# Cosine attention: softmax denominators in four column quarters of TensorE, their inverses spread by transfers

## The chip, the cores and the metric

One NeuronCore of a Trainium2 chip runs the whole program. The metric is the device time of one execution in microseconds (us), lower is better. The engines of the core have queues of their own and meet at semaphores: TensorE (PE, with its weight loads as PEld), VectorE (DVE), ScalarE (ACT), GpSimd (POOL) and SyncE (SP), whose part here is to issue DMA transfers. A run of matmuls on PE works in program order; an instruction that waits holds back all that is behind it on its engine.

## The reference, cut to what matters

The model is a chain of four attention blocks and four feed-forward blocks on x of 16 sequences x 256 tokens x 128 features, all in f32. The change touches the second attention block alone:

```python
q = (x @ w_q).reshape(b, s, h, -1).transpose(0, 2, 1, 3)
...
q = _l2norm(q) * jnp.exp(scale)
k = _l2norm(k)
sim = jnp.einsum('bhid,bhjd->bhij', q, k)
attn = jax.nn.softmax(sim, axis=-1)
out = jnp.einsum('bhij,bhjd->bhid', attn, v)
out = out.transpose(0, 2, 1, 3).reshape(b, s, h * out.shape[-1])
return out @ w_out + b_out
```

There are 16 heads of 64 features; x is layer-normalised ahead of it and the result is added to x. The softmax is worked without its division: the kernel sums exp(sim - peak) over the keys for each query (the denominator) and divides the value product by it.

## The kernel before

The stage is the function `cosine_attention`. Tokens are taken in 8 groups of 512 (two sequences, s = 0 and 1); heads are taken in pairs (r = 0 and 1), 8 pairs to a group, so there are N = 64 pairs of a head pair and a group. Each is numbered n. A software pipeline runs over a step number i. In step i PE does, in this written order: `project(i,0)` (q of pair i, L704), `norm(i-1)` (sums of squares, L717), `score(i-2,0)` (L730), `project_v(i)` (L710), `score(i-2,1)`, `project(i,1)` (k, L704 again), `values(i-3,0)` and `values(i-3,1)` (L744, and L748 for the denominators), then in some steps `turn_x` (four transposes for the next group, L689) or `project_out` of one output tile (L758, L759). An f32 matmul is two instructions in the trace.

The denominators: `consts["ones"]` is all ones, so the matmul at L748 puts the sum over the keys of `summed` on each of its output rows. For each sequence and head it writes 64 rows (the 64 that the head's values take in O_BANK) by 256 columns, so DEN_BANK holds 128 rows x 512 columns that line up with O_BANK. ACT turns them into inverses by Ln and Exp (`invert_den`, L835 and L837, 128x512 each), and DVE multiplies (`normalize`, L905) into `oT`.

The order on the other engines is written out as well. DVE in step i: `take(i,0)` (copies q out of PSUM, L886), `clamp(i-1)` (L892), `normalize(i-4)`, `take(i,1)`, `unite(i-1)` (multiplies q and k by their inverse norms, two instructions at L899), and in output steps `add_out` (L909). In one step of a group `measure` stands ahead of that (L865 to L872), in the next `normalize_x` (L879). ACT in step i: `invert_norm(i-1)` (L805, L811), `exp(i-2,0)`, `copy_v(i)` (L818), `square(i,0)`, `exp(i-2,1)`, `square(i,1)`, `invert_den(i-3)`, and `copy_x` (L795) after `turn_x`; `root` (L786, L788) stands at the head of a step. SP sends in step i the inverse norms of pair i-1: four transfers, each of 32 rows repeated four times into 128 rows of `inv_all` (L670). POOL adds the two key tiles of `probs` into `summed` (L938).

Three waits tie this together. `values(n,0)` waits for `normalized` >= n, that is for `normalize(n-1)`, since O_BANK and DEN_BANK are single. `project(i,1)` waits for `copy_v(i)`, and `project_v(i)` for `take(i,0)`, since all three projections use A_BANK. `take(i,1)` waits for `project(i,1)`.

## Time and profile before

| what | value |
|---|---|
| median of 3 runs | 6622.44 us (6621.18 to 6631.18) |
| profiled execution, its own time | 6623.76 us |
| its span | 6622.0 us |
| cosine stage, first to last instruction on the engines | about 1095 to 1792 us |
| PE busy over the span | 6003.8 us (91%) |
| DVE, ACT, POOL busy over the span | 4160.9, 3471.2, 2272.1 us |

How to read the rows further down. A row of the timeline is: start in us from the span's start, how long in us, engine, line, operation, output<-inputs, rows and columns, count; in brackets the idle time of the engine just before it and what ended it. Consecutive instructions of one line are merged in a row, so the start of one row and the start of the next give the pace of an engine; the length of a row of matmuls takes in the drain of the last of them. A row of the stretches is the stretch, its length, and busy time with instruction count of PE, PEld, DVE, ACT and POOL, then the granted clock of PE as a share of full speed, the busy share of the DMA engines and GB/s. A row of the groups is line, engine, operation, names, shapes and count, then busy us in total and mean ns of one, then idle time before and its releaser. The stage of the change lies wholly on one core, and its steps repeat, so single steps are read.

### The profile page before, as it was taken

To read this page: it belongs to the slowest core of one execution; us is meant where nothing else is said; L and a number is where in the kernel's file an instruction comes from. 1 tells how busy PE (TensorE), PEld (TensorE's weight loads), DVE (VectorE), ACT (ScalarE), POOL (GpSimd) and SP (SyncE) were. 2 spreads that over 40 slices of the span, in tenths; PEclk is the share of its full clock that TensorE was granted. 3 is DMA by queue.
4 is the path that set the end of the run, shared out by engine and by line. 5 is a ranking of instruction groups with operands and counts; after the bars stand their busy time and mean duration, and the time that the engine had idled before them with its cause. 6 is when DMAs were issued, how large, how long until landed. Compare 5 with 4: busy or idle time off the path is not lost. (4 is left out here: it accounts for less than half of the span.)

```text
span 6622.0 us, 128662 instructions
## 1 busy us (share of the span) xinstructions
PE 6003.8 (91%) x51745; PEld 3325.1 (50%) x51745; DVE 4160.9 (63%) x6986; ACT 3471.2 (52%) x5688; POOL 2272.1 (34%) x1589
## 2 busy tenths in 40 slices
PE   7999988999777777999769999999999999999998
PEld 3555554444442223766435555555555555555554
DVE  2333333444358886332768888888888888788885
ACT  3343323666434443444536666666666666666664
POOL 0111100222114443000035555555555555555553
PEclk9999987999968888999879999999999999999998
DMA  1000000222200000000011111111111111111111
GB/s 55 1 1 1 1 0 16 52 52 52 62 5 0 0 0 0 1 0 0 1 45 33 33 46 37 33 46 37 33 43 40 33 40 40 33 35 46 37 38 27
DMA packets 184105, 175.14 MB, mean 26 GB/s; under 512 B 24181, under 2 KB 174742, under 8 KB 183318
## 3 DMA queue, kind: packets, MB, share of 16 engines
q1 hardware_dynamic: 183542, 167.27, 10.6%
q8 instruction: 397, 6.50, 0.4%
q14 instruction: 166, 1.36, 0.1%
HBM read 30.88 MB, written 2.10 MB: 5 GB/s over the span
## 5 line engine op out<-in xcount | busy, mean ns | idle before, releaser
L2545 POOL TENSOR_TENSOR local_ssum<-local_sq 128x512 f32<-128x512 f32 x384 | 694.1, 1808 | 2149.4 <-ACT local_sq L2333 2148.9
L2553 POOL TENSOR_TENSOR local_rot<-local_rot,local_inv_all 128x512 f32<-128x512 f32 x768 | 963.3, 1286 | 87.4 <-DMA local_inv_all<-local_inv 86.7
L2154 PE MATMUL banks<-local_y,local_Wqkv 128*128 128x512 f32 x1536 | 823.4, 618 | 64.2 <-ACT local_sq L2333 61.4
L2355 ACT ACTIVATE local_probs<-local_probs,local_npeak 128x1152 f32<-128x1152 f32 x384 | 482.7, 1257 | 355.2 <-DVE local_probs L2459 355.2
L2459 DVE TENSOR_TENSOR local_probs<-banks,band 128x576 f32<-128x576 f32 x768 | 546.0, 752 | 184.7 <-PE banks L2189 179.3
L2439 DVE TENSOR_TENSOR local_rot<-banks,local_rotary_scaled 128x512 f32<-128x512 f32 x768 | 525.2, 684 | 192.1 <-PE banks L2154 186.4
L2333 ACT ACTIVATE local_sq<-banks 128x512 f32<-128x512 f32 x768 | 459.4, 598 | 246.6 <-DVE local_sin L2440 238.3
L2349 ACT COPY local_v<-banks 128x512 f32<-128x512 f32 x384 | 224.8, 585 | 594.6 <-PE banks L2167 594.1
L2446 DVE TENSOR_TENSOR local_rot<-local_rot,local_sin 128x1024 f32<-128x1024 f32 x384 | 504.9, 1315 | 40.8 <-DVE local_sin L2440 0.9
L2189 PEld LDWEIGHTS banks<-local_rot 32*128 32x128 f32 x12288 | 415.4, 185 | 225.2 <-issue 198.6
L2440 DVE TENSOR_TENSOR local_sin<-banks,local_rotary_scaled 128x512 f32<-128x512 f32 x768 | 521.8, 679 | 0.0
L2209 PEld LDWEIGHTS banks<-local_probs,local_v 128*32 128x32 f32 x12288 | 346.0, 110 | 302.8 <-issue 292.5
L2189 PE MATMUL banks<-local_rot 32*128 32x160 f32 (+1 forms) x12288 | 488.5, 295 | 0.0
L1261 POOL TENSOR_TENSOR mamba_seen<-mamba_state,mamba_c_wide 128x1024 f32<-128x1024 f32 x128 | 301.0, 2352 | 474.9 <-DVE mamba_state L1342 474.9
L2209 PE MATMUL banks<-local_probs,local_v 128*32 128x160 f32 (+1 forms) x12288 | 459.5, 290 | 0.5 <-DVE local_oT L2467 0.5
L2154 PEld LDWEIGHTS banks<-local_y,local_Wqkv 128*128 128x128 f32 x1536 | 264.3, 190 | 371.7 <-ACT local_sq L2333 247.6
L938 POOL TENSOR_TENSOR cosine_summed<-cosine_probs 128x512 f32<-128x512 f32 x128 | 162.7, 1271 | 738.2 <-ACT cosine_probs L828 738.1
L2167 PE MATMUL banks<-local_Wqkv,local_y 128*128 128x512 f32 x768 | 396.0, 597 | 0.0
L419 POOL TENSOR_TENSOR favor_summed<-favor_probs 128x256 f32<-128x256 f32 x128 | 92.9, 726 | 778.1 <-DVE favor_probs L381 778.1
L2224 PE MATMUL banks<-local_oT,local_Wo 128*128 128x512 f32 x768 | 354.9, 605 | 0.9 <-ACT local_gate L2377 0.9
L1158 PE MATMUL banks<-mamba_seen,ident 128*128 128x512 f32 x512 | 291.1, 697 | 63.7 <-DVE mamba_xs L1349 42.3
L381 DVE TENSOR_TENSOR favor_probs<-banks,causal 128x768 f32<-128x768 f32 x128 | 122.6, 957 | 355.3 <-PE banks L231 355.3
(399 smaller groups left out, 10905.1 us busy)
## 6 DMA issues: line engine op xcount, KB each, us to landing
local_inv_all<-local_inv SPq DMA_DIRECT2D x768, 128.0 KB, 2.7
cosine_inv_all<-cosine_inv SPq DMA_DIRECT2D x256, 128.0 KB, 2.6
local_Wqkv<-in_L_ffn_Wqkv_quads SPq DMA_DIRECT2D x36, 256.0 KB, 2.9
local_Wo<-in_L_ffn_Wo_quads SPq DMA_DIRECT2D x6, 512.0 KB, 4.1
experts_w_W<-in_L_ffn_W SPq DMA_DIRECT2D x1, 2048.0 KB
out<-x SPq DMA_DIRECT2D x8, 256.0 KB, 2.3
local_W<-in_L_ffn_W SPq DMA_DIRECT2D x12, 170.5 KB, 2.3
cosine_w_Wqkv<-in_L_attn_w_kv SPq DMA_DIRECT2D x1, 1024.0 KB
```

What stands on the lines that cost most here:

```text
L2154: pe.matmul(seqs(banks[:, QK_BANK, :]), Wqkv[:, at:at + P], y_group(g), start=True, stop=True).then_inc(qk_projected, 1)
L2167: pe.matmul(banks[:, V_BANK, :], y[:, 2 * g + tile // ST, at:at + P], Wqkv[:, V_COLUMNS(half)], start=True, stop=True).then_inc(v_projecte ...
L2189: last = pe.matmul(banks[:, S_BANK + r, lo:hi], k[rows_r, half, at:at + P], q[rows_r, half, at:at + hi - lo], start=(half == 0), stop=(hal ...
L2209: last = pe.matmul(banks[rows_r, O_BANK, part * SEQ + at:part * SEQ + to], v[:, G % 2, s * ST + tile, c:c + 32], probs[:, e % 3, r, lo:hi] ...
L2333: act.activation(sq[:, c % 2, :], banks[:, QK_BANK, :], ACT.Square).then_inc(squared, 1)
L2355: act.activation(a, a, ACT.Exp, bias=npeak[:, layer:layer + 1], scale=SCALE).then_inc(exped, 1)
L2439: dve.tensor_tensor(seqs(rot[:, k % ROTATED, half, :]), raw, twice(table[:, m, 0, half, :]), ALU.mult).then_inc(cosined, 1)
L2440: dve.tensor_tensor(seqs(sin[:, m, half, :]), raw, twice(table[:, m, 1, half, :]), ALU.mult).then_inc(sined, 1)
L2446: dve.tensor_tensor(a, a, sin[:, k % 2, ::-1, :], ALU.add).then_inc(rotated, 1)
L2459: dve.tensor_tensor(probs[:, e % 3, r:r + 2, :], banks[:, S_BANK + r:S_BANK + r + 2, 0:SCORES], consts["band"].unsqueeze(1).broadcast_to([ ...
L2545: pool.tensor_tensor(ssum[:, n % 2, m, :], sq[:, 0, :], sq[:, 1, :], ALU.add).then_inc(square_summed, 1)
L2553: pool.tensor_tensor(a, a, twice(inv_all[:, n % 2, m, of_seq(s)]), ALU.mult).then_inc(united, 1)
```

## The change

The denominators move out of `values` into a function of their own that PE runs after `values(n,1)`. For each sequence s and head r it makes the product with 32 columns of ones, so 32 rows by 256 columns, and puts them at rows 32 x (2s + r) of DEN_BANK: all four of a pair side by side in the four column quarters of the array, in 256 columns of the bank. ACT makes the inverses on 128x256 instead of 128x512, into `inv_den` (two buffers), and does so one step later in the loop, ahead of `invert_norm`, as `invert_den(i-4)`. SP then spreads them: four transfers for each pair, each reading 32 rows twice into the 64 rows of a head for one sequence of `rden` (two buffers now), ahead of the four that send the inverse norms. DVE's `normalize(i-4)` waits for these transfers, and stands behind `take(i,1)` instead of ahead of it. The wait of PE's `values(n,0)` for `normalize(n-1)` stays as it was. `valued` is now counted once a pair and no longer twice, and the waits on it are renumbered.

```diff
...
-        rden, oT = sb("rden", [P, GN]), sb("oT", [P, OUTS, GN])
+        inv_den, rden, oT = sb("inv_den", [P, 2, SEQ]), sb("rden", [P, 2, GN]), sb("oT", [P, OUTS, GN])
...
+        den_sent = signals(nc, ctx, "cos_den_sent_even cos_den_sent_odd")
...
+                def send_den(n):
+                    sp.wait_ge(den_inverted, n + 1)
+                    if n >= 2:
+                        sp.wait_ge(normalized, n - 1)
+                    for q in range(GB):
+                        for r in range(2):
+                            at = 32 * (2 * q + r)
+                            rows = inv_den[at:at + 32, n % 2, :]
+                            source = bass.AP(rows.tensor, rows.offset, [rows.ap[0], [0, 2], rows.ap[-1]])
+                            sp.dma_start(rden[r * HD:(r + 1) * HD, n % 2, of_seq(q)], source).then_inc(den_sent[n % 2], 16)
+
                 for i in range(FIRST, LAST + 1):
+                    if (n := within(i - 4)) is not None:
+                        send_den(n)
                     if (n := within(i - 1)) is not None:
                         send_inverse(n)
...
-                    for r in range(2):
-                        rows_r = slice(r * HD, (r + 1) * HD)
-                        last = pe.matmul(banks[rows_r, DEN_BANK, of_seq(s)], consts["ones"][:, 0:HD], summed[:, n % 2, s, r, :],
-                                         start=True, stop=True)
+
+                def denominators(n):
+                    for s in range(GB):
+                        for r in range(2):
+                            c = 2 * s + r
+                            last = pe.matmul(banks[32 * c:32 * c + 32, DEN_BANK, 0:SEQ], consts["ones"][:, 0:32], summed[:, n % 2, s, r, :],
+                                             start=True, stop=True)
                     last.then_inc(valued, 1)
...
                     if (n := within(i - 3)) is not None:
                         values(n, 0)
                         values(n, 1)
+                        denominators(n)
                     if (g := group_at(i, 2 - PAIRS)) is not None:
...
-                        act.wait_ge(valued, 2 * PAIRS * (g - 1))
+                        act.wait_ge(valued, PAIRS * (g - 1))
...
-                        act.wait_ge(valued, 2 * n - 2)
+                        act.wait_ge(valued, n - 1)
...
                 def invert_den(n):
-                    act.wait_ge(valued, 2 * n + 2)
-                    if n:
-                        act.wait_ge(normalized, n)
-                    act.activation(rden[:], banks[:, DEN_BANK, :], ACT.Ln).then_inc(den_logged, 1)
+                    act.wait_ge(valued, n + 1)
+                    if n >= 2:
+                        act.wait_ge(den_sent[n % 2], 64 * (n // 2))
+                    a = inv_den[:, n % 2, :]
+                    act.activation(a, banks[:, DEN_BANK, 0:SEQ], ACT.Ln).then_inc(den_logged, 1)
                     act.wait_ge(den_logged, n + 1)
-                    act.activation(rden[:], rden[:], ACT.Exp, scale=-1.0).then_inc(rden_ready, 1)
+                    act.activation(a, a, ACT.Exp, scale=-1.0).then_inc(den_inverted, 1)
 
...
                     if (g := group_at(i, 1 - PAIRS)) is not None:
                         root(g)
+                    if (n := within(i - 4)) is not None:
+                        invert_den(n)
...
-                    if (n := within(i - 3)) is not None:
-                        invert_den(n)
                     if (g := group_at(i, 2 - PAIRS)) is not None:
                         copy_x(g)
...
                 def normalize(n):
-                    dve.wait_ge(rden_ready, n + 1)
+                    dve.wait_ge(den_sent[n % 2], 64 * (n // 2 + 1))
                     if n >= OUTS:
                         dve.wait_ge(out_ready, GT * (group_of(n - OUTS) + 1))
-                    dve.tensor_tensor(oT[:, n % OUTS, :], banks[:, O_BANK, :], rden[:], ALU.mult).then_inc(normalized, 1)
+                    dve.tensor_tensor(oT[:, n % OUTS, :], banks[:, O_BANK, :], rden[:, n % 2, :], ALU.mult).then_inc(normalized, 1)
...
                     if (n := within(i - 1)) is not None:
                         clamp(n)
+                    if within(i) is not None:
+                        take(i, 1)
                     if (n := within(i - 4)) is not None:
                         normalize(n)
-                    if within(i) is not None:
-                        take(i, 1)
                     if (n := within(i - 1)) is not None:
                         unite(n)
...
-                        pool.wait_ge(valued, 2 * (n - 2) + s + 1)
+                        pool.wait_ge(valued, n - 1)
...
```

PE's queue at a plain step in the middle of the stage, before (L748 are the denominators, the wait `normalized` is on the first L744 of `values(i-3,0)`):

```order
L704 MATMUL banks<-cosine_xnT,cosine_w_Wqkv 128x512 [waits v_copied]
L744 MATMUL banks<-cosine_probs,cosine_v 64x256 [waits v_copied,normalized,probs_summed,exped]
L744 MATMUL banks<-cosine_probs,cosine_v 64x256 x3
L748 MATMUL banks<-cosine_summed,ones 64x256 x2
L744 MATMUL banks<-cosine_probs,cosine_v 64x256 [waits v_copied,probs_summed,exped]
L744 MATMUL banks<-cosine_probs,cosine_v 64x256 x3
L748 MATMUL banks<-cosine_summed,ones 64x256 x2
```

The same place on PE now, with the line numbers of the changed file (L718 is `project`, L758 `values`, L765 the denominators):

```order
L718 MATMUL banks<-cosine_xnT,cosine_w_Wqkv 128x512 [waits v_copied]
L758 MATMUL banks<-cosine_probs,cosine_v 64x256 [waits v_copied,normalized,probs_summed,exped]
L758 MATMUL banks<-cosine_probs,cosine_v 64x256 x3
L758 MATMUL banks<-cosine_probs,cosine_v 64x256 [waits v_copied,probs_summed,exped]
L758 MATMUL banks<-cosine_probs,cosine_v 64x256 x3
L765 MATMUL banks<-cosine_summed,ones 32x256 x4
```

The two pairs of 64-row denominators became one run of four with 32 rows behind all values; the first of the values still waits for `normalized`.

DVE's queue for one step, before (L886 is `take`, L892 `clamp`, L905 `normalize`, L899 `unite`):

```order
L886 COPY cosine_qk<-banks 128x512 [waits scored,qk_projected]
L892 TENSOR_SCALAR cosine_ss<-banks 128x256 [waits inverted,norm_summed]
L905 TENSOR_TENSOR cosine_oT<-banks,cosine_rden 128x512 [waits out_ready,rden_ready]
L886 COPY cosine_qk<-banks 128x512 [waits scored,qk_projected]
L899 TENSOR_TENSOR cosine_qk<-cosine_qk,cosine_inv_all 128x512 [waits squared,cos_inv_sent_odd]
```

The same place on DVE now (L905 is `take`, L911 `clamp`, L924 `normalize`, L918 `unite`):

```order
L905 COPY cosine_qk<-banks 128x512 [waits scored,qk_projected]
L911 TENSOR_SCALAR cosine_ss<-banks 128x256 [waits inverted,norm_summed]
L905 COPY cosine_qk<-banks 128x512 [waits scored,qk_projected]
L924 TENSOR_TENSOR cosine_oT<-banks,cosine_rden 128x512 [waits out_ready,cos_den_sent_even]
L918 TENSOR_TENSOR cosine_qk<-cosine_qk,cosine_inv_all 128x512 [waits squared,cos_inv_sent_odd]
```

`normalize` changed places with the second `take` of the step.

## Rows read from the trace of the kernel before

**Rows 1.** A stretch in the middle of the stage.

```profile
1400.00:1500.00 100.00, 94.84 (x612) 50.74 (x608) 40.18 (x75) 60.16 (x104) 23.43 (x19) 1.00 0.21 48
```

**Rows 2.** Groups of instructions by line and form, over the stage.

```profile
L748 PE MATMUL banks<-cosine_summed,ones 128*64 128x256 f32 x512 | 77.3, 380 | 0.0
...
L717 PE MATMUL banks<-cosine_sq,heads_of_pair 128*32 128x256 f32 x512 | 41.8, 398 | 3.0 <-ACT cosine_xnT L795 2.9
```

**Rows 3.** Timeline of a plain step, i = 31, PE, DVE and ACT.

```profile
1414.80 1.12 PE L704 MATMUL banks<-cosine_xnT,cosine_w_Wqkv 128*128 128x512 f32 x2
...
1415.86 0.64 PE L717 MATMUL banks<-cosine_sq,heads_of_pair 128*32 128x256 f32 x8
1415.96 0.69 DVE L886 COPY cosine_qk<-banks 128x512 f32<-128x512 f32 x1 [0.77 <-PE banks L704]
...
1416.42 1.13 PE L730 MATMUL banks<-cosine_qk 64*128 64x256 f32 x8
1416.57 0.42 DVE L892 TENSOR_SCALAR cosine_ss<-banks 128x256 f32<-128x256 f32 x1
...
1417.47 0.51 ACT L811 ACTIVATE cosine_inv<-cosine_ss,cosine_up 128x256 f32<-128x256 f32 x1
...
1419.21 0.58 ACT L818 COPY cosine_v<-banks 128x512 f32<-128x512 f32 x1
...
1419.84 1.12 PE L704 MATMUL banks<-cosine_xnT,cosine_w_Wqkv 128*128 128x512 f32 x2 [0.16 <-ACT cosine_v L818]
...
1420.90 1.08 PE L744 MATMUL banks<-cosine_probs,cosine_v 128*64 128x256 f32 x8
1421.00 0.69 DVE L886 COPY cosine_qk<-banks 128x512 f32<-128x512 f32 x1 [3.42 <-PE banks L704]
...
1421.81 0.60 PE L748 MATMUL banks<-cosine_summed,ones 128*64 128x256 f32 x4
...
1422.24 1.03 PE L744 MATMUL banks<-cosine_probs,cosine_v 128*64 128x256 f32 x8
...
1423.11 0.60 PE L748 MATMUL banks<-cosine_summed,ones 128*64 128x256 f32 x4
...
1423.64 1.13 PE L704 MATMUL banks<-cosine_xnT,cosine_w_Wqkv 128*128 128x512 f32 x2
```

**Rows 4.** Timeline, the output step before it, i = 30.

```profile
1403.57 1.12 PE L704 MATMUL banks<-cosine_xnT,cosine_w_Wqkv 128*128 128x512 f32 x2
...
1412.40 2.05 PE L758 MATMUL banks<-cosine_w_Wo,cosine_oT 128*128 128x128 f32 x16
```

**Rows 5.** Timeline, steps i = 32 to 34, where DVE is late.

```profile
1424.20 1.29 DVE L899 TENSOR_TENSOR cosine_qk<-cosine_qk,cosine_inv_all 128x512 f32<-128x512 f32 x2 [2.50 <-DMA cosine_inv_all<-cosine_inv]
...
1434.34 1.12 PE L704 MATMUL banks<-cosine_xnT,cosine_w_Wqkv 128*128 128x512 f32 x2
...
1436.08 1.11 DVE L879 TENSOR_SCALAR cosine_xn<-x,cosine_moments,cosine_rstd 128x128 f32<-128x128 f32 x4 [1.22 <-ACT cosine_rstd L788]
...
1444.77 1.12 PE L704 MATMUL banks<-cosine_xnT,cosine_w_Wqkv 128*128 128x512 f32 x2
```

**Rows 6.** Timeline and the tile `cosine_inv_all`: the transfers of the inverse norms.

```profile
1438.60 0.51 ACT L811 ACTIVATE cosine_inv<-cosine_ss,cosine_up 128x256 f32<-128x256 f32 x1
...
1443.74 1.55 DVE L899 TENSOR_TENSOR cosine_qk<-cosine_qk,cosine_inv_all 128x512 f32<-128x512 f32 x2 [0.92 <-DMA cosine_inv_all<-cosine_inv]
...
L670 SPq DMA_DIRECT2D cosine_inv_all<-cosine_inv x256: 542/604/1417, 1115.1 to 1761.7; - x128
...
DMA to landing us min/median/max: 2.5/2.6/4.3
```

**Rows 7.** Timeline, the end of the stage, where PE waits for `normalize`.

```profile
1774.67 0.69 DVE L905 TENSOR_TENSOR cosine_oT<-banks,cosine_rden 128x512 f32<-128x512 f32 x1 [8.42 <-ACT cosine_rden L837]
...
1775.51 1.08 PE L744 MATMUL banks<-cosine_probs,cosine_v 128*64 128x256 f32 x8 [2.18 <-DVE cosine_oT L905]
```

**Rows 8.** Timeline of PE in the last stage, after an idle stretch.

```profile
3880.98 1.97 PE L2154 MATMUL banks<-local_y,local_Wqkv 128*128 128x512 f32 x2 [2.12 <-ACT local_sq L2333]
```

More of the change, by code:

```diff
@@ L652, in cosine_attention @@
         sems = (qk_projected, copied, squared, norm_summed, clamped, logged, inverted, unit, v_projected, v_copied, scored, exped,
-                probs_summed, valued, den_logged, rden_ready, normalized, out_ready, added) = signals(
+                probs_summed, valued, den_logged, den_inverted, normalized, out_ready, added) = signals(
             nc, ctx, "qk_projected copied squared norm_summed clamped logged inverted unit v_projected v_copied scored exped "
-            "probs_summed valued den_logged rden_ready normalized out_ready added")
+            "probs_summed valued den_logged den_inverted normalized out_ready added")
         inv_sent = signals(nc, ctx, "cos_inv_sent_even cos_inv_sent_odd")
+        den_sent = signals(nc, ctx, "cos_den_sent_even cos_den_sent_odd")
         tiles = lambda g: x[:, g * GT:(g + 1) * GT, :]
@@ L943, in _ @@
                         sum_probs(n, s)
-        restart(nc, [*first, *norms, *sems, *inv_sent])
+        restart(nc, [*first, *norms, *sems, *inv_sent, *den_sent])
 def int4_linear(nc, x, banks, consts, w):
```

## The prediction

> **What bounds the kernel now.** The change lies inside one stage, so I read that stage. The stretch in its middle comes first: PE is busy 94.84 of 100 us at a granted clock of 1.00, the next engine 60 [rows 1]. PE sets the pace there, and PE time saved counts unless a new wait eats it. The groups give the size of what is saved: the denominators keep PE 77.3 us, and the 512 instructions of L717, with the same 256 columns but 32 rows of output each, 41.8 us [rows 2].
>
> Then one plain step in the timeline, T = 1414.80 being its start [rows 3]. PE: project q at T, norm at T+1.06, score at T+1.62, project k at T+5.04, values at T+6.10, denominators at T+7.01, second values at T+7.44, second denominators at T+8.31, next step at T+8.84. Beside it runs one chain: `take` on DVE at T+1.16, `clamp` at T+1.77, Exp of the inverse norms on ACT at T+2.67, `copy_v` at T+4.41, done at T+4.99, and PE goes on at T+5.04 after 0.16 us of idleness. So project k stands at T+5.04 by this chain and nothing in the change shortens it: `invert_den` was done before `clamp` anyway. The second `take` starts at T+6.20, 1.16 us after project k. An output step is the same with 2.40 us more (L758 at 1412.40, next step 1414.80), 11.23 us in all [rows 3, 4].
>
> Where does `normalize` come in? Before, it stands behind `clamp`, finds its inverses ready, and is over by about T+3, long before values at T+6.10. Its wait costs nothing, and no row of the steady state shows PE waiting for it.
>
> **What the change removes: PE time.** L748 takes 0.43 us per pair inside a run (1421.81 to 1422.24) and 0.53 at its end (1423.11 to 1423.64): 0.96 a step. Four products in quarters are what `norm` does: 0.57 us to the next line (1415.86 to 1416.42) [rows 3]. The two values runs take 0.91 and 0.87. So values plus denominators go from 2.74 to 0.91 + 0.87 + 0.57 = 2.35 us, -0.39 a step. Lower bound of the new run is 0.43, half of 2 x 0.43, without any hand-over; upper is 0.67, the 0.57 with another 0.10 as at the end of L748. I take 0.57, the row of the same shape.
>
> On the extra 0.10: the row shows 0.43 for four L748 when 64-row matmuls follow and 0.53 when L704 follows [rows 3]. The Trainium skill (TensorEngine Tiling, Key Properties) says that changing the tiling mode drains the engine. The trace agrees with a tenth of a microsecond. By that rule the change adds one drain a step, from 64-row to 32-row outputs, worth some 6 us over the stage. It leaves the sum as it is but for this.
>
> **What it adds: a wait that PE did not have.** `values(i-3,0)` still waits for `normalize(i-4)`, but DVE now runs that behind `take(i,1)`, and `take(i,1)` waits for project k, the matmul right ahead of values on PE. So PE must stop: project k at T+5.04, `take` starts 1.16 later at T+6.20; the next DVE instruction after a `take` starts 0.61 later (1415.96 to 1416.57), T+6.81; `normalize` lasts 0.69 [rows 3, 7], T+7.50; PE picks up after 0.05 (`copy_v` to L704 [rows 3]) to 0.15 us (1775.36 to 1775.51 [rows 7]); I take 0.10. Values start at T+7.60 instead of T+6.10: +1.50. Queued behind it on PE are all values, denominators and the next step. Rows 7 show the wait itself where `normalize` is late: 2.18 us idle.
>
> Step length: 7.60 + 2.35 = **9.95 us instead of 8.84, +1.11**; an output step gains the same 1.11. The wait applies where there are both a project and an earlier pair, i = 4 to 63, 60 steps: **+67 us**.
>
> **The transfers.** The denominators are ready near T+0.1 of the next step. Ln and Exp on 128x256 take 0.99 us (1416.99 to 1417.98, the norms' pair [rows 3]): T+1.1. The norms' own transfers are the nearest rows: 4.63 us from the end of Exp (1439.11) to `unite` (1443.74) for four issues of 0.604 us [rows 6]. The new ones are half as large each; I take the same 4.63: landed at T+5.7, and `normalize` wants them at T+6.81. Hidden, with 1.1 us to spare. SP is taken for 4 x 0.604 = 2.4 us, to T+3.5, while the norms' inverses are ready at T+3.2: their transfers leave 0.3 later, `unite` starts at T+8.1 and ends by T+9.7; the next `take` is due at T+9.95+1.16 = T+11.1. Hidden too. `score` needs it later still.
>
> A late transfer is not hidden: landing is 2.6 us in the median and 4.3 at worst [rows 6], and one `unite` waited until 6.22 us after its Exp (1417.98 to 1424.20 [rows 3, 5]). That is 1.6 over the usual, 0.5 more than the slack. I estimate one step in four so, 15 x 0.4 = 6 us, and 2 us where `unite` is late: **+8**, between 0 and +30 (every step).
>
> **What it gives back on DVE.** Once in each of six groups `measure` and in the next step `normalize_x` delay `take`: those steps last 10.70 and 10.43 us (1423.64, 1434.34, 1444.77) instead of 8.84 [rows 3, 5]. `normalize_x` starts at T+1.74 because ACT's `root` stands behind `invert_den`; now it stands ahead and needs only `measure`. With DVE 1.4 us earlier in relation to the next `take`, both delays fall under the new slack. Of 1.59 and 1.86 I take 1.59 and 0.8, since in the second a late transfer took part, and 0.4 for `copy_x`, no longer behind `invert_den` (no row; 0 to 0.5). 6 x 2.8 = **-17**, between -10 and -23.
>
> **The end of the stage.** Steps 64 to 67 have no projects to hide behind. PE waits from one run of denominators to the next `normalize`: before, 2.18 us idle [rows 7]. Now 0.1 + 0.99 + 4.63 + 0.69 + 0.10 = 6.5, so +4.3 for each bare hand-over. Two are bare (values of pair 63, the first output), a third partly: **+11**, 8 to 16 with slow first matmuls after it.
>
> **Sum.** 67 + 8 - 17 + 11 = **+69 us**. Against the profiled execution's 6623.76 us that is 6692.8; the median lies 1.3 us lower, so **6691 us**. All other stages are untouched: `restart` clears two more semaphores next to the old ones, nothing. ACT saves some 0.3 us a step off the path, nothing. POOL's new wait (on the whole pair n-2) was long true.
>
> With the low ends: step 9.95 - 0.05 - 0.14 = 9.76, 60 x 0.92 = 55, less 23, no late transfer, +8: +40, 6663. With the high ends: step 10.10, 60 x 1.26 = 76, less 10, +16, late transfers +20: +102, 6725.
>
> **Rivals.** *Transfers pace the step.* If eight transfers a step land later than four did, or two queues of them meet, `normalize` waits for `cosine_rden` and not for `take`. Each step then costs 0.5 more, 60 x 0.5 = 30 in place of the 8: 6713; it decides from a landing 1.1 us later than the norms'. For it: the 1.6 us stragglers. Against: DMA is busy 0.21 of the time [rows 1]. 12%.
>
> *PE's clock drops in the new gaps.* The granted clock is 1.00 in the stage now [rows 1]. In the last stage PE stood idle 2.12 us and the two matmuls after it took 1.97 us, against 1.12 for two of that size here [rows 3, 8]; at the end of this stage PE stood idle 2.18 us and the eight after it took 1.08, as in the middle [rows 3, 7]. So a gap of 2.1 us does either, and mine is 1.5 us, shorter than both. Had the work behind a gap (2.4 us) run at 1.2 in place of 2.4 GHz in every second step, it would be 30 x 2.4 = +72: 6763. 6%. The Trainium skill (TensorE: Matmul & The Clock Gate, A second HAM failure mode) tells of a kernel whose short idlings between runs of matmuls made the clock swing between its levels; by that rule this rival would be the likely one. Rows 7 speak against it at this length.
>
> *Not slower.* If PE's wait were under 0.7 us, the saved 0.39 a step and the 17 us on DVE would outweigh it; with no wait at all, nor the 0.16 us idleness ahead of project k, the stage would give 60 x 0.55 + 17 = 50 back: 6573. It needs `normalize` finished by T+6.8, that is started before `take(i,1)` is over. DVE works in order, and the listing has it behind. 5%. If the four quarters did not run side by side, a step would gain up to 1.1 us more; L717 says they do, 1%.
>
> **How the numbers follow.** Forecast 76%, transfers 12, clock 6, not slower 5, quarters 1. The range 6663 to 6727 takes in the forecast's bounds and the first rival. About 0.2%, 13 us, is what a measurement of this kernel tells from no change: slower by more than that 0.94, faster 0.03, the same 0.03.
>
> **What would show it.** In the profile after: PE idle ahead of the first values (L758 of the new file) with `cosine_oT` as its releaser, about 1.4 us x 60 = 85 us; the denominators' group near 42 us; plain steps of 9.95 and output steps of 12.35 us, none of 10.4 any more among the plain ones from `normalize_x`; `normalize` with no long idle time by DMA; granted clock 1.00. I am wrong if `cosine_oT` releases PE for much less than 80 us, if DVE's idle time by `cosine_rden` passes 15 us, or if the clock falls in the stage.

## The result, and the profile after

The changed kernel takes **6695.84 us** (median of five runs, 6693.89 to 6701.0) against 6625.98 us of the kernel before (five runs, 6621.18 to 6631.18): 1.0107 times as long, with a 95% interval of 1.0092 to 1.0121. That is +69.9 us; forecast were 6691 us and +69. In this section and the next, "after" is the changed kernel.

First the middle of the stage, in the table of stretches. Columns: start and end, length, busy us and instructions of PE, PE's weight loads, DVE, ACT and POOL, then granted clock, share of DMA, GB/s.

```profile
1400.00:1500.00 100.00, 86.95 (x578) 45.30 (x574) 35.99 (x70) 52.32 (x98) 20.77 (x18) 1.00 0.29 68
```

PE was busy 94.84 of the same 100 us before [rows 1]. It now stands still for 13 of them. The clock is granted in full (1.00), so nothing is slower, PE waits. For what, the waits of the stage up to 1830 us tell (engine, line, what was waited for, us in total, times, longest):

```profile
PE banks L758 <- DVE cosine_oT L924: 94.3, 62, 3.4
...
DVE cosine_qk L918 <- DMA cosine_inv_all<-cosine_inv: 37.6, 64, 2.6
...
DVE cosine_oT L924 <- DMA cosine_rden<-cosine_inv_den: 7.7, 2, 4.0
```

The first row is the wait that the change adds: `values` (L758) for `normalize` (L924), 1.47 us in each of 60 steps and longer twice at the stage's end. The third says that the new transfers keep `normalize` waiting twice only, both at the stage's end. Now one plain step of after in the timeline (start, us, engine, line; in brackets the idle time just before and who ended it), the counterpart of [rows 3]:

```profile
1442.05 1.13 PE L718 MATMUL banks<-cosine_xnT,cosine_w_Wqkv 128*128 128x512 f32 x2
...
1446.45 0.58 ACT L836 COPY cosine_v<-banks 128x512 f32<-128x512 f32 x1
...
1447.08 1.13 PE L718 MATMUL banks<-cosine_xnT,cosine_w_Wqkv 128*128 128x512 f32 x2 [0.16 <-ACT cosine_v L836]
...
1448.25 0.69 DVE L905 COPY cosine_qk<-banks 128x512 f32<-128x512 f32 x1 [4.01 <-PE banks L718]
1448.86 0.68 DVE L924 TENSOR_TENSOR cosine_oT<-banks,cosine_rden 128x512 f32<-128x512 f32 x1
...
1449.68 1.95 PE L758 MATMUL banks<-cosine_probs,cosine_v 128*64 128x256 f32 x16 [1.47 <-DVE cosine_oT L924]
1449.86 1.53 DVE L918 TENSOR_TENSOR cosine_qk<-cosine_qk,cosine_inv_all 128x512 f32<-128x512 f32 x2 [0.33 <-DMA cosine_inv_all<-cosine_inv]
...
1451.56 0.64 PE L765 MATMUL banks<-cosine_summed,ones 128*32 128x256 f32 x8
...
1452.13 1.13 PE L718 MATMUL banks<-cosine_xnT,cosine_w_Wqkv 128*128 128x512 f32 x2
```

Read it from T = 1442.05. Project k stands at T+5.03, as before (T+5.04). Then DVE, which had been idle for 4.01 us, takes the keys at T+6.20, and only behind that normalizes the pair before, at T+6.81. PE waits for it from the end of project k and goes on at T+7.63. Both values runs take 1.88 us (1449.68 to 1451.56), all four denominators 0.57, and the next step begins at T+10.08. It was T+8.84. DVE could have run `normalize` within its 4.01 us of idleness, as soon as the transfers had landed; only its place in the listing forbids it. The first experiment shows when they land.

The output steps are as regular, 12.48 us instead of 11.23:

```profile
1404.61 1.13 PE L718 MATMUL banks<-cosine_xnT,cosine_w_Wqkv 128*128 128x512 f32 x2
...
1417.09 1.13 PE L718 MATMUL banks<-cosine_xnT,cosine_w_Wqkv 128*128 128x512 f32 x2
```

The groups by line and form give PE's side of it over the whole stage (busy us, mean ns of one, then idle us before them and their releaser):

```profile
L758 PE MATMUL banks<-cosine_probs,cosine_v 128*64 128x256 f32 x1024 | 127.8, 391 | 100.1 <-DVE cosine_oT L924 100.1
...
L765 PE MATMUL banks<-cosine_summed,ones 128*32 128x256 f32 x512 | 41.3, 394 | 0.0
```

The denominators came down from 77.3 us [rows 2] to 41.3. The saving is real, and 100.1 us of waiting were paid for it, some 88 of them in the 60 steps and the rest at the stage's end. The last view is the end of the stage, where no project hides the transfers:

```profile
1831.80 0.83 PE L765 MATMUL banks<-cosine_summed,ones 128*32 128x256 f32 x8
...
1837.56 0.69 DVE L924 TENSOR_TENSOR cosine_oT<-banks,cosine_rden 128x512 f32<-128x512 f32 x1 [9.23 <-DMA cosine_rden<-cosine_inv_den]
...
1838.40 3.68 PE L758 MATMUL banks<-cosine_probs,cosine_v 128*64 128x256 f32 x16 [5.78 <-DVE cosine_oT L924]
```

From the denominators of one pair to the values of the next PE is idle 5.78 us, where [rows 7] show 2.18, and the values behind so long a pause take 3.68 us for what costs 1.95 above.

The step lengths tell most of the study, so here they are for the five kernels that are compared most, read from the starts of the Exp of the inverse norms, one group of eight steps, in us. The first is that with `measure` in it, the second that with `normalize_x`, the fourth that with `copy_x`; the last four carry an output. Single steps with a late transfer are longer and are not in the table.

| kernel | 1 | 2 | 3 | 4 | 5 to 8 |
|---|---|---|---|---|---|
| before | 9.36 | 10.43 | 8.84 | 9.77 | 11.23 |
| after | 10.08 | 10.08 | 10.08 | 10.48 | 12.48 |
| before, `normalize` behind `take` | 10.38 | 11.97 | 10.38 | 11.30 | 12.78 |
| after, `normalize` ahead of `take` | 9.36 | 9.13 | 8.54 | 8.93 | 11.35, then 10.94 |
| before, `invert_den` behind `root` | 9.36 | 9.13 | 8.84 | 9.23 | 11.23 |

### The profile page after: what moved, and what is told of

The parts are those of the page before. It is cut to its first block and busy times, and to the rows that moved or that the text cites. A ratio compares the mean times of both kernels' runs of the same rounds, so it can differ in the third digit from the quotient of the medians.

```text
span 6692.1 us, 128967 instructions
## 1 busy us (share of the span) xinstructions
PE 5994.5 (90%) x51745; PEld 3319.5 (50%) x51745; DVE 4162.5 (62%) x6986; ACT 3443.3 (51%) x5688; POOL 2271.4 (34%) x1589
```

## The experiments

The theory: the loss is the order on DVE, `normalize` behind `take(i, 1)`, and nothing else of size; the quarters save 0.3 us a step. The rivals: the transfers set the step, or the clock falls in the gaps. The first two experiments are the two halves of the test, each kernel with the other's order on DVE.

**After, with `normalize` ahead of `take` again.**

```diff
                     if (n := within(i - 1)) is not None:
                         clamp(n)
-                    if within(i) is not None:
-                        take(i, 1)
                     if (n := within(i - 4)) is not None:
                         normalize(n)
+                    if within(i) is not None:
+                        take(i, 1)
```

> The changed kernel with one edit: on VectorE normalize(i-4) stands ahead of take(i,1) again. Theory (PE waits for the order on VectorE): the transfers have landed by T+5.2, normalize ends by T+5.9, before values at T+6.10, so PE's wait of 1.47 us goes and a plain step is 6.10 + 1.88 + 0.57 = 8.55 us, an output step 10.95. Against before: 60 x -0.29 = -17, some -4 from ScalarE's order, +12.6 from the end of the stage, where the hand-over by transfers stays bare: about 6618 us, 6608 to 6630. Rival (the transfers themselves, or SyncE, cost the time): it stays above 6650 us, with normalize waiting for cosine_rden.

Measured: 6616.24 us (6614.33 to 6621.95) against 6627.27 of the kernel before on this chip, 0.9986 times, interval 0.9976 to 0.9996. The move alone takes 80 us off after, with all eight transfers in place. A plain step in its timeline:

```profile
1407.00 1.12 PE L718 MATMUL banks<-cosine_xnT,cosine_w_Wqkv 128*128 128x512 f32 x2
...
1409.61 0.69 DVE L924 TENSOR_TENSOR cosine_oT<-banks,cosine_rden 128x512 f32<-128x512 f32 x1 [0.42 <-DMA cosine_rden<-cosine_inv_den]
...
1412.04 1.12 PE L718 MATMUL banks<-cosine_xnT,cosine_w_Wqkv 128*128 128x512 f32 x2 [0.16 <-ACT cosine_v L836]
1413.10 1.95 PE L758 MATMUL banks<-cosine_probs,cosine_v 128*64 128x256 f32 x16
...
1415.54 1.13 PE L718 MATMUL banks<-cosine_xnT,cosine_w_Wqkv 128*128 128x512 f32 x2
```

The step is 8.54 us, 0.30 under before, and the values have no idle time ahead of them. `normalize` now does wait for its transfers:

```profile
DVE cosine_oT L924 <- DMA cosine_rden<-cosine_inv_den: 126.6, 64, 9.3
...
PE banks L758 <- DVE cosine_oT L924: 16.1, 10, 5.8
```

64 waits of DVE, 126.6 us in all, of which 16.1 us reach PE: 12.5 in three waits at the stage's end and 3.6 in seven steps, mostly the first output step of a group, where PE waits 0.33 to 0.97 us. The step above follows an output step, so its transfers had 2.4 us more than usual. Behind a plain step the margin is small:

```profile
1435.36 1.13 PE L718 MATMUL banks<-cosine_xnT,cosine_w_Wqkv 128*128 128x512 f32 x2
...
1440.37 0.69 DVE L924 TENSOR_TENSOR cosine_oT<-banks,cosine_rden 128x512 f32<-128x512 f32 x1 [2.82 <-DMA cosine_rden<-cosine_inv_den]
...
1441.45 1.95 PE L758 MATMUL banks<-cosine_probs,cosine_v 128*64 128x256 f32 x16
```

The transfers have landed at T+5.01, `normalize` is over at T+5.70, and values start at T+6.09. So DVE waits for the transfers, but in a plain step PE does not. The rival "transfers pace the step" is excluded for this order, and so for after, where there is more time still.

**Before, with `normalize` behind `take`.** Nothing else of the change.

```diff
                     if (n := within(i - 1)) is not None:
                         clamp(n)
-                    if (n := within(i - 4)) is not None:
-                        normalize(n)
                     if within(i) is not None:
                         take(i, 1)
+                    if (n := within(i - 4)) is not None:
+                        normalize(n)
```

> The kernel before with one edit: on VectorE normalize(i-4) stands behind take(i,1); no quarters, no transfers of denominators. Theory: PE waits as in the changed kernel, values start at T+7.63 instead of T+6.10, a plain step is 10.37 us: 60 x 1.53 = +92, less some 5 for VectorE's measure: +87, 6713 us (6705 to 6720), slower than the changed kernel. Rival (the transfers or the quarters are the cause): 6626 us.

Measured: 6717.5 us (6716.59 to 6718.91), 1.0136 times, interval 1.0119 to 1.0153. Without one new transfer the wait is there, with the same length as in after:

```profile
1222.92 0.69 DVE L886 COPY cosine_qk<-banks 128x512 f32<-128x512 f32 x1 [4.02 <-PE banks L704]
1223.53 0.68 DVE L905 TENSOR_TENSOR cosine_oT<-banks,cosine_rden 128x512 f32<-128x512 f32 x1
1224.35 1.08 PE L744 MATMUL banks<-cosine_probs,cosine_v 128*64 128x256 f32 x8 [1.47 <-DVE cosine_oT L905]
```

The plain step goes from 8.84 to 10.38, +1.54: that is the order by itself. From here to after, 10.08, is -0.30: the quarters by themselves. Both numbers come out the same from the other side (10.08 to 8.54 is 1.54, 8.84 to 8.54 is 0.30), so in a plain step the two effects simply add. Over the whole kernel they do not: the swap is worth 90.2 us here and 79.6 us between after and the run above, because PE's wait also hides delays (of `measure`, of `normalize_x`, of late transfers), and in after it hides more of them. The second step of a group shows the third part: `normalize_x` makes it 11.97 here and 10.08 in after, 1.59 more than the 0.30. Most of that comes from the order on ACT, as the next experiment shows.

**Before, with ACT's new order alone.**

```diff
                     if (g := group_at(i, 1 - PAIRS)) is not None:
                         root(g)
+                    if (n := within(i - 4)) is not None:
+                        invert_den(n)
...
-                    if (n := within(i - 3)) is not None:
-                        invert_den(n)
```

> The kernel before with one edit: on ScalarE invert_den moves to the next step, behind root and ahead of invert_norm. Theory (the part of the gain that comes from ScalarE's order): the step with normalize_x loses 1.25 of its 1.6 us delay and the step behind turn_x 0.4: 6 x 1.7 = -10, 6616 us (6613 to 6620). Rival (VectorE's delays stem from late transfers, not from root): no change, 6626 us.

Measured: 6615.95 us (6610.37 to 6619.71), 0.9983 times, interval 0.9973 to 0.9992; in the traces the span goes from 6622.0 to 6611.6 us. Step 2 becomes 9.13 instead of 10.43 and step 4 becomes 9.23 instead of 9.77, 1.84 a group. `normalize_x` no longer waits for ACT's `root` (1.22 us in [rows 5]):

```profile
1429.70 1.12 PE L704 MATMUL banks<-cosine_xnT,cosine_w_Wqkv 128*128 128x512 f32 x2
1430.14 1.11 DVE L879 TENSOR_SCALAR cosine_xn<-x,cosine_moments,cosine_rstd 128x128 f32<-128x128 f32 x4
...
1438.83 1.13 PE L704 MATMUL banks<-cosine_xnT,cosine_w_Wqkv 128*128 128x512 f32 x2
```

**After, with longer transfers.** Each of the four transfers of the inverse denominators is first made into a spare tile, so that the last real one comes four issues later; the spare ones are work that the kernel does not use. The counts that are waited for double with them.

```diff
+        spare = sb("spare", [P, 2, GN])
...
+                            sp.dma_start(spare[r * HD:(r + 1) * HD, n % 2, of_seq(q)], source).then_inc(den_sent[n % 2], 16)
                             sp.dma_start(rden[r * HD:(r + 1) * HD, n % 2, of_seq(q)], source).then_inc(den_sent[n % 2], 16)
```

> The changed kernel with each of the four denominator transfers issued twice, once into a spare tile, all of them waited for. Theory (the transfers are hidden with 1.7 us to spare in plain steps and more behind output steps): the last lands near T+7.45, 0.7 past the 6.81 at which normalize could start: 32 x 0.7 = +22 and some 7 at the end, 6725 us, and steps behind an output step keep 12.48 us. Rival (transfers pace every step): +2.4 us in each of 60 steps, over 6830 us.

Measured, in a single run: 6772.07 us, 76 more than after and 47 more than expected. A step that follows a plain one:

```profile
1493.11 0.69 DVE L926 TENSOR_TENSOR cosine_oT<-banks,cosine_rden 128x512 f32<-128x512 f32 x1 [0.70 <-DMA cosine_rden<-cosine_inv_den]
1493.95 3.55 PE L760 MATMUL banks<-cosine_probs,cosine_v 128*64 128x256 f32 x16 [2.27 <-DVE cosine_oT L926]
```

The transfers do what they were expected to: with 2.4 us more of issues `normalize` is 0.70 us late, which leaves a slack of some 1.7 us in after where the prediction counted 1.1. The rest is something else. PE's gap is 2.27 us instead of 1.47, and the values behind it take 3.55 us instead of 1.95. The table of stretches for this step and its neighbour:

```profile
1485.50:1497.90 12.40, 9.97 (x58) 4.63 (x54) 4.91 (x16) 6.33 (x13) 2.53 (x2) 0.86 0.35 85
1497.90:1509.80 11.90, 9.48 (x58) 4.00 (x54) 4.10 (x9) 6.03 (x11) 2.53 (x2) 0.92 0.37 89
```

The granted clock is 0.86 and 0.92 there: of the two levels, 2.4 and 1.2 GHz, PE has the lower one for part of the step. This is the clock rival, which after escaped. It is not all of the difference. The 60 steps are 62 us longer than those of after. Of that, 27 us are longer gaps ahead of the values (22 were expected) and 19 us the values runs themselves, 18 of which are slow. Some 6 us are waits of PE behind late inverse norms, whose transfers stand behind eight others here, and some 10 us were not told apart. The end is another 14 us longer. By how much after escaped the clock is a question for two more kernels.

**After, with one multiplication more on DVE ahead of `normalize`.** It multiplies a constant tile of 128x512 by itself into a spare tile (work that the kernel does not use) and makes the gap longer without touching a transfer.

```diff
                     if within(i) is not None:
                         take(i, 1)
+                        for k in range(1):
+                            dve.tensor_tensor(extra[:, k, :], ones4, ones4, ALU.mult)
                     if (n := within(i - 4)) is not None:
                         normalize(n)
```

> The changed kernel with one VectorE multiply of 128x512 (0.61 us to the next instruction) put between take(i,1) and normalize(i-4). It touches no transfer. Its result is not used. Theory: PE's gap grows from 1.47 to 2.08 us, plain steps from 10.08 to 10.69: +37 us, 6733 us, as long as the granted clock stays 1.00. If the clock falls in gaps of this length as it did behind gaps of 2.27 us with doubled transfers, up to 1.6 us more in each such step, 6733 to 6830 us. Rival (the drop of the clock there came with the transfers, not with the gap): 6733 us and a clock of 1.00.

Measured, in a single run: 6760.5 us. The wait itself is worth what was expected: 10.69 us in an undisturbed plain step, 13.09 with an output, +0.61 each. But 20 of the 60 steps are longer than that, mostly by 1.6 us. Two output steps, one after the other, with the same gap:

```profile
1456.03 1.95 PE L760 MATMUL banks<-cosine_probs,cosine_v 128*64 128x256 f32 x16 [2.08 <-DVE cosine_oT L926]
...
1469.12 3.63 PE L760 MATMUL banks<-cosine_probs,cosine_v 128*64 128x256 f32 x16 [2.08 <-DVE cosine_oT L926]
```

Sixteen matmuls take 1.95 us behind one gap of 2.08 us and 3.63 behind the next. The granted clock of just these two stretches is 1.00 and 0.50:

```profile
1456.10:1457.90 1.80, 1.80 (x16) 1.16 (x16) 1.46 (x2) 0.00 (x0) 0.31 (x1) 1.00 0.00 0
1469.20:1472.60 3.40, 3.40 (x16) 2.00 (x16) 1.44 (x2) 0.00 (x0) 0.29 (x1) 0.50 0.03 5
```

The 20 steps explain some 30 us, and 60 x 0.61 another 37, about the 66 us by which this kernel's span exceeds that of after.

**After, with two such multiplications.** As above with `range(2)`.

> The same with two such multiplies: PE's gap is 2.69 us. By the wait alone 60 x 1.22 = +73, 6769 us. Theory (the clock falls behind gaps above some 2 us): the values behind the gap take 3.5 instead of 1.9 us in most steps, 6830 to 6900 us, granted clock in the stage below 0.95. Rival (the clock does not follow the gap): 6769 us.

Measured, in a single run: 6967.51 us, above all that was expected. Its timeline in an ordinary step:

```profile
1358.47 2.35 DVE L947 TENSOR_TENSOR cosine_extra<-inside 128x512 f32<-128x512 f32 x2
1358.60 1.68 POOL L961 TENSOR_TENSOR cosine_summed<-cosine_probs 128x512 f32<-128x512 f32 x1 [1.07 <-ACT cosine_probs L848]
...
1361.57 3.54 PE L760 MATMUL banks<-cosine_probs,cosine_v 128*64 128x256 f32 x16 [3.74 <-DVE cosine_oT L926]
```

The gap is 3.74 us rather than the intended 2.7, because the two multiplications take 2.35 us where the single one took 0.68. They lie beside POOL's sum, which itself takes 1.68 us instead of 1.27. So this kernel says nothing on a gap of 2.7 us. It says that behind 3.74 us all 60 values runs are slow, 59 of them over 3 us:

```profile
1400.00:1500.00 100.00, 74.85 (x402) 35.68 (x400) 40.35 (x69) 42.26 (x78) 19.76 (x14) 0.85 0.23 54
```

**Before, with the denominators grouped but not in quarters.** Does it help to put the four denominators behind both values runs, with 64 rows each as before?

```diff
-                    for r in range(2):
-                        rows_r = slice(r * HD, (r + 1) * HD)
-                        last = pe.matmul(banks[rows_r, DEN_BANK, of_seq(s)], consts["ones"][:, 0:HD], summed[:, n % 2, s, r, :],
-                                         start=True, stop=True)
-                    last.then_inc(valued, 1)
+                def denominators(n):
+                    for s in range(GB):
+                        for r in range(2):
+                            rows_r = slice(r * HD, (r + 1) * HD)
+                            last = pe.matmul(banks[rows_r, DEN_BANK, of_seq(s)], consts["ones"][:, 0:HD], summed[:, n % 2, s, r, :],
+                                             start=True, stop=True)
+                    last.then_inc(valued, 2)
...
                         values(n, 1)
+                        denominators(n)
```

> The kernel before with its four 64-row denominator products behind both values, as in the changed kernel, but not in quarters. Theory (the array time falls because four products run at once, not because they stand together): a plain step stays 8.84 us within 0.05, values 1.78 and denominators 0.96 us, 6626 us. Rival (fewer hand-overs between values and denominators are what saves): 0.2 us or more less a step, 6614 us or less.

Measured, in a single run: 6634.4 us beside a kernel before of 6628.94 (6623.04 to 6632.88), so no gain; the steps are 8.84 and 11.23 as in before. Its timeline:

```profile
1442.66 1.95 PE L744 MATMUL banks<-cosine_probs,cosine_v 128*64 128x256 f32 x16
1444.43 1.03 PE L751 MATMUL banks<-cosine_summed,ones 128*64 128x256 f32 x8
1445.40 1.13 PE L704 MATMUL banks<-cosine_xnT,cosine_w_Wqkv 128*128 128x512 f32 x2
```

Values 1.77 us, denominators 0.97. In after the same values take 1.88 us when 32-row matmuls follow. So the 0.30 that a step saves is 0.40 from the quarters less 0.1 for the change of shape, and grouping gives none of it.

**After, with `normalize` ahead and the last four pairs without transfers.** After with `normalize` ahead of `take`, and the last four pairs with 64-row denominators whose Ln and Exp write the inverses straight into `rden`, without a transfer.

```diff
+    DIRECT = N - 4
...
+                    if n >= DIRECT:
+                        for s in range(GB):
+                            for r in range(2):
+                                last = pe.matmul(banks[r * HD:(r + 1) * HD, DEN_BANK, of_seq(s)], consts["ones"][:, 0:HD], summed[:, n % 2, s, r, :],
+                                                 start=True, stop=True)
+                        last.then_inc(valued, 1)
+                        return
...
+                    if n >= DIRECT:
+                        act.wait_ge(normalized, n - 1)
+                        a = rden[:, n % 2, :]
+                        act.activation(a, banks[:, DEN_BANK, :], ACT.Ln).then_inc(den_logged, 1)
+                        act.wait_ge(den_logged, n + 1)
+                        act.activation(a, a, ACT.Exp, scale=-1.0).then_inc(den_direct, 1)
+                        return
```

> The changed kernel with normalize(i-4) ahead of take(i,1), and the last four pairs, n = 60 to 63, made as in the kernel before: 64-row products over the whole bank, Ln and Exp on 128x512 straight into rden, no transfers. Theory: in the steady state the quarters save 0.29 us a step, and the bare hand-overs by transfers at the stage's end give back 12 us; without them 6616 - 11 = 6605 us (6600 to 6610), faster than the kernel before and than either run with one order changed. Rival (the end costs for another reason, the slower clock or the outputs): no change from 6616 us.

Measured: 6608.77 us (6607.37 to 6612.65) against 6628.94, 0.9971 times, interval 0.996 to 0.9983. It is 20 us faster than the kernel before and 87 faster than after. Of the two parts, the end is the visible one. From the last Exp of the inverse norms (1737.55) to the end of the last addition (1773.94) are 36.4 us, where the previous version, the same but for the end, takes 46.6 and before 33.4. PE waits as in [rows 7]:

```profile
1753.81 0.69 DVE L943 TENSOR_TENSOR cosine_oT<-banks,cosine_rden 128x512 f32<-128x512 f32 x1 [8.04 <-ACT cosine_rden L865]
1754.64 1.95 PE L760 MATMUL banks<-cosine_probs,cosine_v 128*64 128x256 f32 x16 [2.18 <-DVE cosine_oT L943]
```

It is 4 us above the expected 6605 and inside the stated range. The 60 steps take what they took in the version without the new end (598.3 against 597.9 us), and the end gives back 10 us of the 11 expected; the remaining difference lies outside the stage, where no work was changed.

## Why the prediction was right

The main step held: what PE gains from denominators in quarters is lost several times over, because `normalize` was put behind a `take` that waits for the matmul just ahead of `values`. The terms, one by one:

- **The wait**, forecast +1.50 us a step: +1.54 by the swap of two calls in either kernel. In after the values stand at T+7.63 and not T+7.60, as PE picks `normalize` up after 0.14 us; the mean of 0.05 and 0.15 was taken, and the row with DVE as releaser [rows 7] was the right one.
- **PE's work**, forecast -0.39: -0.30. The denominators are the 0.57 us of the forecast. The step that was off is the values run, taken as 0.91 + 0.87 = 1.78 and measured 1.88. The Trainium skill (TensorEngine Tiling (Array Packing), Key Properties) says that a change of tiling mode drains the engine; the prediction named it, priced it at 6 us and left it out of the sum. The trace agrees with the rule: 1.88 us with 32-row matmuls behind, 1.77 with 64-row ones. In the sum it would have made +75.
- **Step**, forecast 9.95 and 12.35 us: 10.08 and 12.48. Over 60 steps that is +74 instead of +67.
- **Late transfers**, forecast +8: nothing. No step of after is longer than its kind, 10.09 us for a plain one, 10.48 with `copy_x` and 12.49 with an output, and the tile `cosine_rden` shows:

```profile
DMA to landing us min/median/max: 2.1/2.1/3.7
```

  The prediction took for the small transfers the 4.63 us of the large ones from Exp to use. The half as large ones land in 2.1 us where those take 2.6 [rows 6], and with `normalize` ahead it starts 4.04 us behind the Exp (1436.33 to 1440.37). Ln and Exp took 0.83 us, not 0.99. Together that gives a slack of some 1.8 us, and the longest landing, 1.6 over the median, did not use it up. On top of this the inverse norms had stragglers of 4.3 us before; in after the longest took 3.0.
- **What DVE and ACT give back**, forecast -17: -19. Per group 0.52 in step 1, 1.59 in step 2 and 0.53 in step 4, 2.64 together, in six groups, 0.65 in one step ahead of them, and some 3 us of late steps that after does not have. Whether its longer slack or its lack of stragglers spares it these, the runs do not separate. The forecast for the three was 0.8, 1.59 and 0.4.
- **The end**, forecast +11: +12.6. The bare pauses are 5.78 us and not 6.5, so +3.6 each and not +4.3; the first matmuls behind them are slow, as was said, and make up for it.
- **Sum**: steps 4 to 63 take 55.3 us more (forecast 58), the end 12.6 more (11), and 2 us stand ahead of step 4, where no work differs. 69.9 against 69 is so close because two misses cancelled: the step came out 7 us dearer, mostly by the drain, and the late transfers 8 us cheaper.

The prediction said it would be wrong if DVE's idle time by `cosine_rden` passed 15 us. It is 26.5 us over the stage, in four waits, all at its end: 4.0 and 3.7 and then 9.23 and 9.54, idle time with nothing else to do, while the steps' own share is nothing. The sign was badly worded; it should have been asked of the 60 steps.

The rival **not slower**, had `normalize` stood ahead, was put at 6573 us. That experiment gave 6616. Its step was valued at 0.55 us of gain with the 0.16 us ahead of project k; it gained 0.30, because the `copy_v` gap stays whatever is done to the denominators and because of the drain. The 17 us that DVE and ACT were to give back shrank to 2: the 60 steps are 20 us shorter than before, and 18 of them are 60 x 0.30. With no wait on PE, `measure` keeps its step at 9.36 us, and late transfers make single steps as long as 11.98. It also left out the stage end: from the last Exp of the inverse norms to the last addition before takes 33.4 us, after 46.2 and after with `normalize` ahead 46.6, so these 13 us are the transfers' price whichever order DVE has.

The rival **clock** did not come about in after, and was nearer than 6% suggests. The Trainium skill (TensorE: Matmul & The Clock Gate, A second HAM failure mode) tells of short idlings that make the clock swing. The traces agree where gaps of 2.08 us stand in each step, and not in after: none of its 60 gaps of 1.47 us is followed by a slow values run. Before with the swapped order has the same gap and two such runs in 60, this the first:

```profile
1201.26 1.98 PE L744 MATMUL banks<-cosine_probs,cosine_v 128*64 128x256 f32 x8 [1.47 <-DVE cosine_oT L905]
```

Eight matmuls take 1.98 us instead of 1.08, and from this Exp to the next are 11.79 us instead of 10.38. In both cases it stands in the step with `normalize_x`, where PE had already stood idle 0.74 us ahead of `project_v` and 0.94 us ahead of project k. The run with doubled transfers has a third: values of 3.46 us behind a gap of 1.47, with pauses of 1.22, 0.49 and 0.94 us before it in that step. After has no such step, as ACT's new order and the slack take those pauses away. That is a likely reason why it kept clear, but no run tests it, and four of the six such steps of the swapped kernel ran at full clock too.

The length of the gap alone does not decide either. At the end of after's stage PE stood idle for 3.42 us and ran at full speed behind it:

```profile
1820.18 1.95 PE L758 MATMUL banks<-cosine_probs,cosine_v 128*64 128x256 f32 x16 [3.42 <-DVE cosine_oT L924]
```

The next values, behind a gap of 2.49 us, took 3.39.

Also open is why some transfers of the inverse norms land late. Their longest landing is 4.3 us in before, in after with `normalize` ahead and in the combined version, 4.6 in before with ACT's order, 3.0 in after and 3.3 in before with the swapped order; but 4.2 in after with one multiplication more, where PE has a gap too. Neither the number of transfers nor the gap sorts them. One thing goes with them: the longest single issue of these transfers on SP is 0.68 us in after and 1.26 to 1.97 us in all nine other kernels, where 0.60 is usual. What holds these issues up is not shown.

## What to carry to other kernels

Engines run their lists in order, so a step's price is read from what stands ahead of it on its own engine and who waits for the result: two calls in the wrong order on DVE, idle 4 us just before, cost 1.54 us a step here, 80 to 90 us in all, four to five times the 18 us that the better matmuls saved. When a change brings several edits, swap the one that looks like mere order in both kernels; if the two differences agree, as they do here in the plain steps, the parts add there and each has its price. A small new gap on PE is to be judged with its margin as well: 0.6 us more of it cost nearly as much again through the clock as through the waiting.

## What the runs showed of the hardware

- **Clock.** With one pattern of work, PE gaps of 1.47 us were followed by a slow run in 0 of 60 steps (after) and in 2 of 60 (before with the order swapped, both behind further pauses of 0.74 and 0.94 us), of 2.08 us in 20 of 60, and of 3.74 us in 60 of 60; the sixteen values matmuls then take up to 3.68 us instead of 1.95, with a granted clock of 1.00, 0.98 to 1.00, 0.93 to 0.97 and 0.81 to 0.85 over stretches of 100 us of the stage. Single gaps of 3.42 (after) and 2.98 us (after with `normalize` ahead) at the stage's end were followed by none.
- **Changing the output rows of a matmul** costs PE some 0.10 us: 64-row values followed by 32-row denominators 1.88 us, followed by 64-row ones 1.77.
- **Quarters run side by side for f32 with 256 columns**: 0.57 us for four products, against 0.97 with 64 rows each in two halves.
- **DVE beside POOL.** A multiplication of SBUF tiles of 128x512 that began just ahead of POOL's sum of the same size took 0.68 us; with a second right behind it, beside the sum, the two took 2.35. The sum took 1.68 instead of 1.27 in both kernels. The kernel's own `unite` shows it mildly: 1.29 us alone, 1.53 to 1.65 beside POOL in after.
- **Landing of small transfers** from SBUF to SBUF: half the size, with half as many rows written, saves half a microsecond, as the page of after has it (KB, then median us to landing):

```profile
cosine_inv_all<-cosine_inv SPq DMA_DIRECT2D x256, 128.0 KB, 2.6
cosine_rden<-cosine_inv_den SPq DMA_DIRECT2D x256, 64.0 KB, 2.1
```
